# Forming the low part of a tile's input on VectorE in the inner slots as well, in place of GpSimd

## The reference, cut to what matters

```python
h = _layernorm(x, axis=-1) * (1 + ca) + sa
x = x + ga * attention(h, Wq, Wk, Wv, Wo, bo, ...)
h = _layernorm(x, axis=-1) * (1 + cb) + sb
x = x + gb * ffn(h, base_W, base_b, shared_A, shared_B, routed_A, routed_B, router_W, router_b)
# attention, of one batch:
q = _rope(x @ Wq); k = _rope(x @ Wk); v = x @ Wv
a_win = _masked_softmax(q4 @ k4.T * SCALE, (cols <= rows) & (cols > rows - 128))
```

## Time and profile before

| | |
|---|---|
| median of the runs | 2371.56 us |
| the profiled execution, its own time | 2375.0 us |
| span of the profile | 2373.1 us |
| PE busy | 2145.7 us (90%) |
| DVE busy | 1749.7 us (74%), 4740 instructions |
| ACT busy | 1340.7 us (56%) |
| POOL busy | 788.2 us (33%), 780 instructions |
| mean granted clock of PE | 0.962 of full speed |
| chain that ended last | PE 63%, DVE 22%, ACT 6%, issue 5%, POOL 2% |

### The profile page before, as it was taken

One profiled execution on the slowest core, in us unless ns is written; L12 is line 12 of the kernel. 1 busy time (PEld: TensorE's weight loads), 2 busy tenths in 40 slices (PEclk: granted clock), 3 DMA queues, 4 the chain that ended last, 5 costly groups with the idle time before them and its releaser, 6 DMA issues.

```text
span 2373.1 us, 48974 instructions
## 1 busy us (share of the span) xinstructions
PE 2145.7 (90%) x17944; PEld 1427.3 (60%) x17944; DVE 1749.7 (74%) x4740; ACT 1340.7 (56%) x4701; POOL 788.2 (33%) x780
## 2 busy tenths in 40 slices
PE   4888999899998999989999899989999899997887
PEld 0665666566665666656665566656666566664454
DVE  3456888768886788768887688866887678875776
ACT  1244666556665566646656566655666556663664
POOL 0333333343333233333332433324333423333221
PEclk9998999999999999989999899999999999997989
DMA  6010000200011000110001100020001100011000
GB/s 233 19 40 15 23 28 24 68 22 28 28 32 63 28 24 28 46 49 19 28 28 41 54 28 24 23 76 24 22 25 45 50 28 28 24 46 45 19 19 19
DMA packets 48892, 89.64 MB, mean 38 GB/s; under 512 B 6760, under 2 KB 6760, under 8 KB 48656
## 3 DMA queue, kind: packets, MB, share of 16 engines
q1 hardware_dynamic: 39440, 69.74, 9.6%
q10 hardware_dynamic: 9216, 16.78, 1.9%
HBM read 69.68 MB, written 16.83 MB: 36 GB/s over the span
## 4 chain that ended last, share of the span: by engine, by line
PE 63%; DVE 22%; ACT 6%; issue 5%; POOL 2%; DMA 1%; SPq 0%; DVEq 0%; ACTq 0%; POOLq 0%
PE ps_m L702 9%; PE ps_o L634 7%; PE ps_m L506 6%; PE ps_m L667 5%; PE ps_m L507 5%; PE ps_m L508 5%; PE ps_s L628 4%; PE ps_t L610 4%; DVE ps_s L1548 4%; ACT pw L1033 3%; PE ps_m L684 3%; DVE wmax L1553 3%; PE ps_s L597 3%; PE ps_s L586 3%; PE ps_m L705 2%
## 5 line engine op out<-in xcount | busy, mean ns | idle before, releaser
L1033 ACT ACTIVATE pw<-ps_s,wmax 128x128 f32<-128x128 f32 x1024 | 360.3, 382 | 168.5 <-DVE wmax L1553 168.4
L506 PE MATMUL ps_m<-w_hi,h_hi 128*128 128x512 f32 x768 | 374.0, 487 | 35.1 <-DVE rbf L1520 18.9
L1043 ACT ACTIVATE pw<-pw,wden 128x128 f32<-128x128 f32 x1024 | 313.2, 401 | 5.0 <-DVE wden L1563 4.8
L507 PE MATMUL ps_m<-w_lo,h_hi 128*128 128x512 f32 x768 | 309.7, 403 | 0.0
L508 PE MATMUL ps_m<-w_hi,h_lo 128*128 128x512 f32 x768 | 308.5, 402 | 0.0
L1067 ACT ACTIVATE pT<-ps_s 80x512 f32<-80x512 f32 (+7 forms) x240 | 141.9, 591 | 255.6 <-PE ps_o L634 155.7
L1311 POOL TENSOR_TENSOR h_lo<-hT,h_hi 128x512 fp32r<-128x512 f32 x57 | 72.3, 1268 | 540.4 <-ACT h_hi L993 540.4
L702 PE MATMUL ps_m<-wbt_s,h2T 128*128 128x512 f32 x512 | 249.0, 604 | 0.0
L667 PE MATMUL ps_m<-wo_s,aT 128*128 128x512 f32 x512 | 247.8, 609 | 0.0
L1574 DVE COPY_PREDICATED pT<-keep_prev,ps_t 128x512 f32<-128x512 uint32 x224 | 164.3, 733 | 94.2 <-PE ps_t L610 90.2
L1033 ACT ACTIVATION_READ_ACCUMULATOR pw<-ps_s,wmax 128x1 f32 x1024 | 226.6, 221 | 0.0
(11 more groups left out here) (187 smaller groups left out, 4341.9 us busy)
## 6 DMA issues: line engine op xcount, KB each, us to landing
xa<-x_in SPq DMA_DIRECT2D x65, 256.0 KB, 3.0
xc<-x_in SPq DMA_DIRECT2D x64, 256.0 KB, 2.8
out<-t ACTq DMA_DIRECT2D x64, 256.0 KB, 2.0
wo_s<-wo_in SPq DMA_DIRECT2D x8, 1024.0 KB, 6.3
wbt_s<-wbt_in SPq DMA_DIRECT2D x8, 1024.0 KB
gbc<-gate_rows SPq DMA_DIRECT2D x24, 256.0 KB, 5.4
pw<-wmod_in SPq DMA_DIRECT2D x3, 1024.0 KB, 5.5
pT<-wmod_in SPq DMA_DIRECT2D x3, 1024.0 KB, 5.3
```

Source lines behind the costliest of these rows:

```text
L506: pe_.matmul(ps[:], h_hi[:, c, :], w_hi[:, col, c, :], start=(c == 0), stop=False)
L507: pe_.matmul(ps[:], h_hi[:, c, :], w_lo[:, col, c, :], start=False, stop=False)
L1033: ins = act.activation(pw[:, hw, :], ps_w[:, j, i, 1, :], ACT.Exp, bias=wmax[:, hw:hw + 1], accum_out=wden[:, 0, hw:hw + 1])
L1043: act.activation(pw[:, hw, :], pw[:, hw, :], ACT.Copy, scale=wden[:, 2, hw:hw + 1]).then_inc(wn_ok, 1)
```

## The change

In `slot`, the call `split_h(Ta)` leaves POOL's list, and a call `split_low(Ta)` enters DVE's list behind `cs_max` and ahead of `window_max` of half 0. Nothing else changes. The semaphores are the same, the arithmetic too.

```diff
@@ gpsimd, slot @@
                 t, ba = s - 1, b + 1
                 Ta = NT * ba + t
-                split_h(Ta)
                 residual_in(b, t)
                 cs_subtract(b, s)
@@ vector, slot @@
                 cs_mask(b, s)
                 cs_max(b, s)
+                split_low(Ta)
                 window_max(b, s, 0)
                 residual(seg, b, t)
                 window_weights(b, s, 0)
```

## The result

The changed kernel takes 2386.19 us (median of three, 2385.5 to 2386.3), against 2371.56 before: +14.6 us. The ratio on record is 1.0056, 95% interval 1.0042 to 1.0070 (the two medians by themselves give 1.0062). In a later set, beside the kernel before on one chip, it was 1.0086 (1.0072 to 1.0099). The forecast was 2391.8 us with a range of 2380 to 2401, the ratio 1.0085. Its profiled execution took 2385.5 us.

The account below looks back on a forecast made before the run. The prediction took the start of Q's rotation on DVE to set each inner slot's length. Slots s = 2 to 7 add 18.8 us, `residual_in` 1.4: 2371.6 + 20.2 = 2391.8 us, range 2380 to 2401.

Parts of the forecast that it names:

- (a): Slot s = 2 without a conflict between DVE's subtraction and POOL: `window_max` starts 0.74 us later.
- (b): Slot s = 2 with DVE's subtraction held until POOL's `cs_subtract` is through: `window_max` starts 1.10 us later; the case taken.
- the hold in s = 2 and 4: DVE's two-SBUF-input subtraction waits for POOL's running instruction, then still takes 0.55 us; s = 4 is like s = 2.
- Rival 1: The wide subtraction on DVE is not held by POOL: 14.7 us slower, 2386.3 us; chance 0.17.
- (c): Slot s = 3: DVE gets in between POOL's two instructions; `window_max` starts 0.80 us later, 0.74 without the conflict.
- rival 3: POOL keeps the SBUF side between two queued instructions, so DVE waits for the second too: 2407.2 us; chance 0.07.
- (d): Slot s = 5: DVE goes on before POOL's semaphore has come, and loses 0.61 us.
- rival 2: Delay absorbed between maxima and rotation, only gains in s = 6 and 7 remain: 3.6 us faster, 2368.0 us; chance 0.08.
- rival 4: Low part ready sooner, so Q's projection starts sooner: at most 25 us faster, 2346 us; chance 0.02.
- (e): Slots s = 6 and 7: POOL's subtraction no longer holds a small DVE instruction; `window_max` 0.39 and 0.12 us earlier.
- (f): `residual_in` now right behind POOL's last call: nothing in 35 slots, +0.2 us at each of seven first slots, 1.4 us.
- The sum: Total over seven batches: 18.8 us from slots s = 2 to 7 plus 1.4 us from `residual_in`, 20.2 us slower.

Follow-up runs that it names:

- experiment 5: Changed kernel with DVE's subtraction behind `window_max` and PE's wait for the low part moved to the first product that reads it: 2369.62 us, ratio 0.9982.
- experiment 6: Changed kernel with DVE's subtraction behind `window_max`, PE's wait kept at the start of Q's projection: 2399.85 us, ratio 1.0110.
- experiment 1: Changed kernel with one wait added on POOL, so `cs_subtract` starts only when the low part is written: 2382.71 us, ratio 1.0042.
- experiments 2 and 7: Kernel before with POOL's `residual_in` ahead of `split_h` in inner slots: 2372.42 us; only in s = 6, 7, `split_h` also waiting for DVE's maxima: 2359.84 us.
- experiment 3: Kernel before with `residual_in` ahead of `split_h`, and in s = 6 and 7 POOL's subtraction waiting for DVE's maxima: 2364.23 us, ratio 0.9951.

## Why the prediction was right

- **Which engine holds the slot.** Right. The start of Q's rotation on DVE sets it, and `h_lo` does not: PE's wait for `h_lo` stayed at POOL's 14 places in the changed kernel. It became late only behind `window_max`, in 22 places in experiment 5 and in all 42 inner slots in experiment 6.
- **(a), (b), the hold in s = 2 and 4.** Right: in s = 2 `window_max` starts 1.10 us later, and 0.73 without the overlap (experiment 1), for 1.10 and 0.74; the slot is 0.92 to 0.95 us longer for 0.96. Choosing the row of a 6-column instruction for a 512-column one was sound here. Rival 1, whose 2386.3 us happens to lie on the first measurement, is refuted by L1678's 1.05 us and by experiment 1. A total that fits is no proof of its mechanism.
- **(c), s = 3.** Right, +0.65 for 0.66, and DVE did get in between POOL's two instructions; rival 3 falls.
- **(d), s = 5.** +0.49 to +0.52 for 0.61. `window_max` did start 0.61 us later, the rotation of Q only 0.55: there is a little slack here as well, which the sum took off in s = 2 to 4 alone. Another 0.04 is the one odd slot in the profile before.
- **The other rivals.** Nothing was absorbed in s = 2 to 5 (rival 2), and an earlier `h_lo` gave nothing (rival 4).
- **(e), the gain in s = 6 and 7.** Right, -0.49 and -0.22 for -0.39 and -0.12. The split started 0.09 behind L1599's start and not 0.13, so the rotation starts 0.43 and 0.17 us earlier; the last 0.05 of each is the odd slot in s = 6 and, in s = 7, arises in the turn and is not traced. These small terms times seven are why 18.8 us became 16.1 and 17.0.
- **(f), `residual_in`.** Nothing in 35 slots, as said. L1489 after a first slot took 1.49 us, as said, and the piece behind it is 0.25 to 0.3 us longer with it than without (experiments 2 and 7), for 0.2: some 2 us in all, for 1.4. In the total it drowned in the clock.
- **The place.** The prediction says that the loss comes from standing ahead of the exponentials. Experiment 5 shows it for most of the loss: same work, same engine, behind them, and the inner slots lose some 5 us in place of 16 to 17. It does not turn into a gain there; the total under before comes from PE's moved wait in the turns and the prologue, and from the clock.
- **The sum.** 20.2 us against 14.6 and, in the second set, 20.4 by its ratio. What the code did is 16.1 to 17.0 us in the inner slots and turns and some 2 around the first slots, 18 to 19; the rest, either way, is the clock. That the second set comes within 0.2 us of the forecast is luck. Between the profiled executions the difference is 10.5, because the one before had the long epilogue; by the loop alone it is 15.0 and 18.2.

## What to carry to other kernels

Before moving an operation off an "idle" engine onto the busier one, find out what its new place stands in front of: here 0.7 us of work, ahead of a reduction that ACT was waiting for, cost the kernel 0.6% to 0.9%; behind it, the inner slots lost a third of what they had lost ahead of it, and only with PE's wait put at the first product that reads the result. When an edit moves two things, take the pieces apart: the second of them, the wait, was worth some 7 us in places that the first doesn't touch. Look at the longest record of small instructions, not only at their mean: a maximum of 1.21 us for an instruction of 0.18 pointed to the collision whose removal, one wait on POOL, gave 0.5%. And compare slot by slot where the code differs; in a total of 2370 us some 4 us of clock can hide effects of 0.1 us per slot.

## What the runs showed of the hardware that I had not expected

- A DVE instruction with two SBUF inputs of 512 columns was held by POOL's instruction and then needed 0.55 of its 0.69 us, in s = 2; POOL in turn waited for DVE and its pair was stretched from 1.64 to 2.07 us in s = 3. That holding goes both ways was known from the earlier trace rows; that a waiting DVE gets in between two queued POOL instructions was so in all seven batches (0.77 us each time). DVE's COPY_PREDICATED on PSUM is not held: in experiment 3 it ran its 1.29 us beside POOL's L1311.
- The first product after a wait costs PE some 0.1 us beyond the wait (the next starts 0.31 us behind it in place of 0.23), and by my estimate the head start of about 0.2 us that it otherwise gets under the last products of the group ahead. With the wait just behind the first two products (experiment 5) a slot was 0.5 us shorter than with the wait ahead of them.
- Unchanged code behind a long wait of PE took 25.4 us at a mean granted clock of 0.81 and 22.9 at 0.92 in one slot of the epilogue, and the whole epilogue was 3.8 to 6.2 us shorter in eight of nine profiles than in the one before. Between executions of one kernel the mean clock differed too (0.961 to 0.968). At this size an effect of 0.2% in the total can't be given to an edit without the timeline.
